# Query and key factors of the first attention: three Newton steps on DVE in place of a power on POOL

## The chip, the cores and the metric

The kernel runs on one core of a Trainium2 chip. A core has a matrix engine (PE, whose weight loads are listed as PEld), a vector engine (DVE), an activation engine (ACT), a general engine (POOL, also called GpSimd) and a queue engine (SP). Each engine works through its own list of instructions in order, and the lists are tied together by semaphores. The metric is the device time of one execution in microseconds (us), lower is better. A partition is one of 128 rows of on-chip memory; "128x24" is 24 elements in each of 128 partitions.

## The reference, cut to what matters

Two transformer-like layers run one after the other on 16 batches of 512 tokens with 128 channels. The change lies in the first attention:

```
h = rmsnorm(layernorm(x)) * norm_w
q = h @ Wq   (4 heads of 32)        k = h @ Wk   (2 heads of 32)
q = q / max(||q||, 1e-12)           k = k / max(||k||, 1e-12)      per token and head
attn = softmax(causal(q . k * exp(log_temperature)));   out = attn @ v @ Wo
x = x + xn + gate * out + experts(xn)
```

The divisions by a norm are what is touched: for each token and each of the 4 + 2 heads one factor 1/sqrt(max(sum of squares, 1e-24)) is made and multiplied in. A batch has 512 tokens in 4 tiles of 128, so the factors of a batch are a 128x24 tile. The rms norm is folded in: `r2` is its factor per token, `r2sq` its square, and the sum of squares is scaled by it first.

## The kernel before, in words

The program has six stages in a row: set-up, first attention with routing (`layer0_attention`), a table of groups, 80 groups of experts, the second attention, and again a table and groups of experts. Only the first attention is changed. It is pipelined by hand over the 16 batches `b`. Each engine has its own loop, written out in the order in which it shall work, and it is this order that decides what waits for what.

- PE in turn `b`: `scores(b, 0)` to `scores(b, 3)` (L632, L635), with the transposes and projections of batch b+2 between them; then `output(b-1)` (L658), which waits for `norm_done` from `normalise(b-1)`; `values(b, 0)` (L647); `q_columns(b+1)` (L588), which waits for `wo_used` from `add_output(b-1)`; `k_columns(b+1)`, `ranks(b+1)` (L610), and the rest of the scores and values.
- ACT in turn `b`: the exponentials of the scores, the copies of batch b+2, and last `squares(b+2)` (L523), the squares of its queries and keys.
- DVE in turn `b`: `normalise(b-1)` (a reciprocal L403 and a product `a_attnT` L405), `statistics(b+3)`, `heads_rows(b+1)` (L344: queries times factors `a_fac`), `add_output(b-1)` (L411), `choose(b+1)` (L357 to L372), `keep_sum`, `slots(b+1)` (L378 to L397), `normal_rows(b+3)` (L323, which needs `rstd` from POOL) and `square_sums(b+2)` (L336: the 128x24 sums `a_ss`).
- POOL in turn `b`: `scatter(b, 0)` (four indirect DMAs, L487), `norms(b+3)` (L458 to L464: `rstd`, `r2`, `r2sq`), `scatter(b, 1)`, and `factors(b+2)` (L474 to L479: product, maximum, power -0.5, product).

A `Chain` counts instructions of one engine: `fc.link(ins)` lets `ins` raise a semaphore and the engine wait for it before its next instruction. An instruction issued without `link` is not waited for. Where the buffers of a batch are named: `ftmp` is the scratch of the factors, `fac` the result.

Of the kernel before, what the change touches and what calls it, by code (L numbers as in the profile page):

```python
# [14 lines left out]
P = 128  # L15
# [181 lines left out]
def layer0_attention(nc, k, x_d, base_d, meta_d, xs_d):  # L197
# [4 lines left out]
    with ExitStack() as ctx:  # L202
# [11 lines left out]
        prj = sb("a_prj", [P, 2, NT, PRJ0])  # L214
        sq = sb("a_sq", [P, NT * (H0 + KV0), DH0])
        ss = sb("a_ss", [P, NT, H0 + KV0])
        ftmp = sb("a_ftmp", [P, 3, NT, H0 + KV0])
        fac = sb("a_fac", [P, NT, H0 + KV0])
        qn = sb("a_qn", [P, NT, D])
        kn = sb("a_kn", [P, NT, D])  # L220
# [37 lines left out]
        s_ps, exp_done, pv_tile = sem("a_s_ps"), sem("a_exp"), sem("a_pvt")  # L258
        norm_done, wo_ps, wo_used = sem("a_norm"), sem("a_wo_ps"), sem("a_wo_used")
        base_out = [sem(f"a_base_out{p}") for p in range(2)]  # L260
        dve_ln, dve_qkv, dve_main, pool_ln, pool_fac = (sem(f"a_{n}") for n in ("dve_ln", "dve_qkv", "dve_main", "pool_ln", "pool_fac"))

        def done(eng, sem, count):

            if count > 0:
                eng.wait_ge(sem, count)
# [5 lines left out]
        with nc.Block() as block:  # L272
# [29 lines left out]
            def _(dve):  # L302
                ln = Chain(dve, dve_ln, 1)
                heads = Chain(dve, dve_qkv, PRO_DVE_A)
                main = Chain(dve, dve_main, 1)

                def statistics(b):
                    ln.at(b)
                    dve.wait_ge(x_in[b % RX], 16 * (b // RX + 1))
                    done(dve, rstd_ready, b)  # L310
                    for t in range(NT):
                        last = nc.vector.bn_stats(stats[:, t, :], x[:, b % RX, t, :])
                    ln.link(last)
                    for t in range(NT):
                        last = nc.vector.bn_aggr(mv[:, t, :], stats[:, t, :])
                    last.then_inc(stats_ready, 1)
                    ln.end()
# [15 lines left out]
                def square_sums(b):  # L333
                    dve.wait_ge(sq_ready, b + 1)
                    done(dve, fac_ready, b)
                    nc.vector.tensor_reduce(ss[:].rearrange("p t h -> p (t h)"), sq[:], AX, ALU.add).then_inc(ss_ready, 1)  # L336

                def heads_rows(b):
                    heads.at(b)
# [34 lines left out]
                def slots(b):  # L374

                    dve.wait_ge(rank_ps, b + 1)
                    for t in range(NT):
                        nc.vector.tensor_tensor(pos[:, t], ps_p[:, RT + t * E0:RT + (t + 1) * E0], k.run0[:], ALU.add)  # L378
                        last = nc.vector.tensor_tensor(k.run0[:], ps_p[:, RT + (NT + t) * E0:RT + (NT + t + 1) * E0],
                                                       k.run0[:], ALU.add)  # L380
                        if t < NT - 1:
                            heads.link(last)
                    last.then_inc(rank_used, 1)
                    dve.wait_ge(rank_used, b + 1)
                    for c in range(2):
                        last = nc.vector.tensor_tensor(ohp[:, c], oh[:, c], pos[:], ALU.mult)
                    heads.link(last)
                    heads.link(nc.vector.tensor_reduce(slotf[:].rearrange("p c t -> p (c t)"),
                                                       ohp[:].rearrange("p c t e -> p (c t) e"), AX, ALU.add))
                    dve.wait_ge(el_ready, b + 1)  # L390
                    done(dve, meta_out[b % 2], 16 * (b // 2))
                    scatter_done(dve, b - 2)
                    heads.link(nc.vector.tensor_scalar(ep[:], el[:], 1.0, None, ALU.add))
                    wts = meta[:, b % 2].bitcast(F32)
                    heads.link(nc.vector.reciprocal(wts[:, 2 * NT:3 * NT], ep[:]))
                    nc.vector.tensor_tensor(wts[:, 3 * NT:4 * NT], el[:], wts[:, 2 * NT:3 * NT], ALU.mult)
                    nc.vector.tensor_copy(meta[:, b % 2, 0:2 * NT], slotf[:].rearrange("p c t -> p (c t)")).then_inc(meta_ready, 1)  # L397
                    heads.end()
# [17 lines left out]
                statistics(1)  # L416
                normal_rows(1)
                square_sums(0)
                statistics(2)
                heads_rows(0)  # L420
                normal_rows(2)
                choose(0)
                square_sums(1)
                slots(0)
                keep_sum(0)
                for b in range(NB):
                    if b >= 1:
                        normalise(b - 1)
                    if b + 3 < NB:
                        statistics(b + 3)  # L430
                    if b + 1 < NB:
                        heads_rows(b + 1)
                    if b >= 1:
                        add_output(b - 1)
                    if b + 1 < NB:
                        choose(b + 1)
                        keep_sum(b + 1)
                        slots(b + 1)
                    if b + 3 < NB:
                        normal_rows(b + 3)  # L440
                    if b + 2 < NB:
                        square_sums(b + 2)
                normalise(NB - 1)
                add_output(NB - 1)

            @block.gpsimd
            def _(pool):
                ln = Chain(pool, pool_ln, 6)
                fc = Chain(pool, pool_fac, 3)

                def norms(b):

                    ln.at(b)
                    pool.wait_ge(stats_ready, b + 1)
                    done(pool, xn_ready, b)
                    done(pool, fac_ready, b - 1)
                    done(pool, qkv_ready, b - 2)
                    ln.link(nc.gpsimd.tensor_scalar(tmp4[:, 0], mv[:, :, 1], EPS_LN, None, ALU.add))  # L458
                    ln.link(nc.gpsimd.tensor_tensor(rstd[:], tmp4[:, 0], k.mhalf[:, 0:NT], ALU.pow))
                    ln.link(nc.gpsimd.tensor_tensor(tmp4[:, 1], rstd[:], rstd[:], ALU.mult))  # L460
                    ln.link(nc.gpsimd.tensor_tensor(tmp4[:, 2], tmp4[:, 1], mv[:, :, 1], ALU.mult))
                    ln.link(nc.gpsimd.tensor_scalar(tmp4[:, 0], tmp4[:, 2], 1e-6, None, ALU.add))
                    ln.link(nc.gpsimd.tensor_tensor(r2[:, b % RN], tmp4[:, 0], k.mhalf[:, 0:NT], ALU.pow))
                    nc.gpsimd.tensor_tensor(r2sq[:, b % 2], r2[:, b % RN], r2[:, b % RN], ALU.mult).then_inc(rstd_ready, 1)  # L464
                    ln.end()

                def factors(b):

                    fc.at(b)
                    pool.wait_ge(ss_ready, b + 1)  # L470
                    pool.wait_ge(rstd_ready, b + 1)
                    done(pool, qkv_ready, b)
                    bc = r2sq[:, b % 2].unsqueeze(2).to_broadcast([P, NT, H0 + KV0])
                    fc.link(nc.gpsimd.tensor_tensor(ftmp[:, 0], ss[:], bc, ALU.mult))  # L474
                    fc.link(nc.gpsimd.tensor_scalar(ftmp[:, 1], ftmp[:, 0], 1e-24, None, ALU.max))
                    fc.link(nc.gpsimd.tensor_tensor(ftmp[:, 2].rearrange("p t h -> p (t h)"),
                                                    ftmp[:, 1].rearrange("p t h -> p (t h)"),
                                                    k.mhalf[:, 0:NT * (H0 + KV0)], ALU.pow))
                    nc.gpsimd.tensor_tensor(fac[:], ftmp[:, 2], r2[:, b % RN].unsqueeze(2).to_broadcast([P, NT, H0 + KV0]),  # L479
                                            ALU.mult).then_inc(fac_ready, 1)  # L480
                    fc.end()

                def scatter(b, c):
                    if c == 0:
                        pool.wait_ge(meta_ready, b + 1)
                    for t in range(NT):
                        nc.gpsimd.indirect_dma_start(  # L487
                            xs_d, bass.IndirectOffsetOnAxis(ap=meta[:, b % 2, c * NT + t:c * NT + t + 1], axis=0),
                            xn[:, b % RX, t, :], None).then_inc(scattered[b % 2], 16)

                norms(0)
                norms(1)
                factors(0)
                norms(2)
                factors(1)
                for b in range(NB):
                    scatter(b, 0)
                    if b + 3 < NB:
                        norms(b + 3)
                    scatter(b, 1)  # L500
                    if b + 2 < NB:
                        factors(b + 2)
                for p in range(2):
                    pool.wait_ge(scattered[p], SCAT * (NB // 2))

# [1489 lines left out]
```

## Time and profile before

| what | value |
|---|---|
| median of 3 runs | 1691.02 us (1690.0 to 1691.55) |
| profiled execution, its own time | 1692.21 us |
| its span (first to last instruction) | 1690.5 us |
| mean granted PE clock | 0.943 of full speed |
| busy over the span | PE 89%, DVE 69%, ACT 56%, POOL 50% |
| first attention | starts at about 12 us; its last DVE instruction ends at 351.15 us |

The busy shares are means over six stages with different limits; the change concerns only the first fifth of the span. Within it the rows of a timeline give the start of each instruction or run of instructions, how long it was, and in brackets how long its engine had been idle before it and what ended the wait.

### The profile page before, as it was taken

How to read it: one execution, taken by the hardware profiler on the slowest of the kernel's cores; microseconds unless marked ns; L12 is line 12 of the kernel's file. 1: busy time of each engine (PE TensorE's matmuls, PEld its weight loads, DVE VectorE, ACT ScalarE, POOL GpSimd, SP SyncE). 2: the span in 40 equal slices, each digit the busy share in tenths (PEclk: the TensorE clock that was granted, in tenths of full speed). 3: DMA queues.
4: the chain of work that ended last, by engine and by line, in shares of the span. 5: the costliest groups of instructions: out<-in, count | busy, mean ns of one | idle time of the engine just before them, and what ended most of it. 6: DMA issues, size and time to landing. Idle time of an engine off the chain costs nothing. (4 is left out here: it accounts for less than half of the span.)

```text
span 1690.5 us, 29816 instructions
## 1 busy us (share of the span) xinstructions
PE 1500.7 (89%) x9488; PEld 778.3 (46%) x9488; DVE 1174.4 (69%) x3105; ACT 941.4 (56%) x1805; POOL 844.9 (50%) x989
## 2 busy tenths in 40 slices
PE   3999998939996299999999999999999999639996
PEld 1444444429996133333333333333333333129996
DVE  3677777633333478989888898889988999224443
ACT  2555555514442137777777777777777777512221
POOL 4788888806001654556554655556555520104443
PEclk9999999959998559999999999999999999959998
DMA  1111111159998211122212221122211210067771
GB/s 34 50 53 51 58 57 46 52 160 277 300 299 241 68 52 47 55 75 72 62 46 62 76 61 55 56 71 75 64 52 55 67 57 5 26 214 233 237 239 64
DMA packets 141519, 165.75 MB, mean 98 GB/s; under 512 B 28010, under 2 KB 114154, under 8 KB 140138
## 3 DMA queue, kind: packets, MB, share of 16 engines
q1 hardware_dynamic: 86628, 70.75, 14.5%
q10 hardware_dynamic: 40912, 62.62, 12.0%
q0 software_dynamic: 13824, 30.47, 5.9%
q8 instruction: 78, 1.28, 0.3%
q14 instruction: 77, 0.63, 0.1%
HBM read 111.93 MB, written 51.30 MB: 97 GB/s over the span
## 5 line engine op out<-in xcount | busy, mean ns | idle before, releaser
L1529 DVE TENSOR_REDUCE c_mx<-c_ps_mx 128x1 f32<-128x512 f32 x1024 | 648.3, 682 | 86.9 <-PE c_ps_mx L1757 83.5
L1435 ACT ACTIVATE c_pt<-c_ps_e 128x512 f32<-128x512 f32 x1024 | 555.5, 602 | 198.0 <-PE c_ps_e L1729 193.5
L1757 PE MATMUL c_ps_mx<-c_kex,c_qst 72*128 72x512 bf16 x1024 | 399.4, 392 | 17.7 <-DVE c_mx L1529 9.4
L1729 PE MATMUL c_ps_e<-c_qst,c_kex 74*128 74x512 bf16 x1024 | 389.8, 383 | 1.7 <-ACT c_pt L1435 1.6
L1742 PE MATMUL c_ps_v<-c_pt,c_vp 128*32 128x512 f32 x2048 | 274.5, 608 | 1.1 <-ACT c_pt L1435 0.7
L1272 POOL DMA_INDIRECT c_gy<-ys,mt x128 | 124.3, 971 | 276.2 <-DMA mt<-meta 128.0
L1757 PEld LDWEIGHTS c_ps_mx<-c_kex,c_qst 72*128 72x128 bf16 x1024 | 100.9, 99 | 332.0 <-DVE c_mx L1529 230.0
L985 PE MATMUL f_ps_h<-f_xT,f_w 128*128 128x256 f32 x800 | 196.5, 385 | 0.0
L545 ACT ACTIVATE a_pt<-a_ps_s,temp 128x1024 f32<-128x1024 f32 (+3 forms) x128 | 113.1, 885 | 92.8 <-PE a_ps_s L635 90.4
L985 PEld LDWEIGHTS f_ps_h<-f_xT,f_w 128*128 128x128 f32 x800 | 145.4, 194 | 15.4
L487 POOL DMA_INDIRECT xs<-a_xn,a_meta x128 | 133.4, 1042 | 35.1 <-issue 32.6
L995 PEld LDWEIGHTS f_ps_y<-f_w,f_h 128*128 128x128 f32 x1120 | 144.5, 193 | 6.2
L995 PE MATMUL f_ps_y<-f_w,f_h 128*128 128x128 f32 x1120 | 144.7, 275 | 0.0
L938 POOL DMA_INDIRECT out<-f_y,f_x x80 | 76.8, 960 | 130.1 <-DVE f_y L1068 117.6
L1365 POOL DMA_INDIRECT rows<-c_row,c_bsl x64 | 64.0, 999 | 155.1 <-PE c_ps_v L1742 123.8
L1729 PEld LDWEIGHTS c_ps_e<-c_qst,c_kex 74*128 74x128 bf16 x1024 | 100.4, 98 | 72.7 <-ACT c_pt L1435 16.7
L1016 ACT ACTIVATE f_h<-f_ps_h,f_w 128x256 f32<-128x256 f32 x160 | 68.3, 474 | 88.8 <-PE f_ps_h L985 87.9
L1012 ACT ACTIVATE f_g<-f_ps_h 128x256 f32<-128x256 f32 x120 | 46.1, 384 | 120.9 <-PE f_ps_h L985 101.6
L632 PE MATMUL a_ps_s<-a_qT,a_kT 32*128 32x128 f32 (+3 forms) x512 | 108.4, 500 | 0.3
L973 PE MATMUL f_ps_x<-ident,f_x 128*128 128x128 f32 x240 | 47.3, 280 | 63.3 <-DMA f_x<-rows 39.7
L1072 DVE TENSOR_TENSOR f_y<-f_ps_y,f_w 128x256 f32<-128x256 f32 x80 | 33.9, 424 | 98.7 <-PE f_ps_y L995 98.7
L1060 DVE TENSOR_TENSOR f_h<-f_ps_h,f_g 128x256 f32<-128x256 f32 x120 | 50.9, 425 | 66.8 <-ACT f_g L1012 66.8
(225 smaller groups left out, 1898.8 us busy)
## 6 DMA issues: line engine op xcount, KB each, us to landing
f_w<-in_we ACTq DMA_DIRECT2D x80, 321.0 KB, 4.5
f_w<-in_we ACTq DMA_DIRECT2D x40, 576.0 KB, 4.4
c_qst<-qparts SPq DMA_DIRECT2D x45, 384.0 KB
f_x<-rows SPq DMA_DIRECT2D x40, 257.0 KB, 3.9
f_x<-xs SPq DMA_DIRECT2D x80, 128.0 KB, 4.6
ys<-f_y ACTq DMA_DIRECT2D x80, 128.0 KB, 4.3
qparts<-c_qp SPq DMA_DIRECT2D x16, 384.0 KB, 2.5
c_kex<-kparts SPq DMA_DIRECT2D x48, 96.0 KB
```

The costliest lines, as they stand in the source:

```text
L487: nc.gpsimd.indirect_dma_start(xs_d, bass.IndirectOffsetOnAxis(ap=meta[:, b % 2, c * NT + t:c * NT + t + 1], axis=0), xn[:, b % RX, t, :], ...
L545: nc.scalar.activation(pt[:, kt % 2, 2 * pr:2 * pr + 2, 0:n], ps_s[:, u % 2, :, 0:n], ACT.Exp, bias=k.temp[:, 3:4], scale=k.temp[:, 1:2]). ...
L632: nc.tensor.matmul(ps_s[:, u % 2, j, 0:L - kt * P], kT[r, b % 2, kt * P:(kt + 1) * P], qT[r, b % 2, kt * P:L], start=True, stop=False)
L938: nc.gpsimd.indirect_dma_start(ys_d, bass.IndirectOffsetOnAxis(ap=x[:, q, t, 2 * D:ROW].bitcast(U32), axis=0), y[:, q, t, :], None).then_i ...
L985: last = nc.tensor.matmul(ps_h[u][:, n, :], w[:, q, col:col + P], xT[:, q % 2, :], start=True, stop=True)
L995: last = nc.tensor.matmul(ps_y[q % 2][:, t * D:(t + 1) * D], h[:, q % 2, c, t * P:(t + 1) * P], w[:, q, col:col + D], start=c == 0, stop=c ...
L1272: nc.gpsimd.indirect_dma_start(gy[:, p, n, :], None, ys_d, bass.IndirectOffsetOnAxis(ap=mt[:, p, n:n + 1], axis=0)).then_inc(gathered[p], 16)
L1435: nc.scalar.activation(pt[:, s % 4, hl, :], ps_e[:, ring_bank(p, n)], ACT.Exp, scale=QSCALE).then_inc(exp_done, 1)
L1529: nc.vector.tensor_reduce(mx[:, g % 2, n % 16:n % 16 + 1], ps_mx[:, ring_bank(p, n)], AX, ALU.max).then_inc(mx_done, 1)
L1729: nc.tensor.matmul(ps_e[:, ring_bank(p, n)], kex[:, p, hl, kt * P:(kt + 1) * P], qst[:, p, HL * g + hl, :], start=True, stop=True).then_in ...
L1742: last = nc.tensor.matmul(ps_v[32 * hl:32 * (hl + 1), :], vp[:, p, kt, hl, :], pt[:, s % 4, hl, :], start=kt == 0, stop=kt == NT - 1)
L1757: nc.tensor.matmul(ps_mx[:, ring_bank(p, n)], qst[0:SROW, p, HL * g + hl, qt * P:(qt + 1) * P], kex[0:SROW, p, hl, :], start=True, stop=Tr ...
```

## The change

The four POOL instructions of `factors` go away, in the loop and twice ahead of it. Fourteen DVE instructions on 128x24 tiles take their place, right behind the sums of squares: the product with `r2sq`, the maximum, an integer guess of 1/sqrt (the bits read as an integer, times -0.5, plus a constant), the halved negative, three Newton steps of three instructions, and the product with `r2`. Each waits for the one ahead of it through a semaphore, with one exception: the halved negative is issued right behind the guess.

```diff
@@ -214,7 +214,7 @@
-        ftmp = sb("a_ftmp", [P, 3, NT, H0 + KV0])
+        ftmp = sb("a_ftmp", [P, 4, NT, H0 + KV0])
@@ -258,7 +258,7 @@
-        dve_ln, dve_qkv, dve_main, pool_ln, pool_fac = (sem(f"a_{n}") for n in ("dve_ln", "dve_qkv", "dve_main", "pool_ln", "pool_fac"))
+        dve_ln, dve_qkv, dve_main, pool_ln, dve_fac = (sem(f"a_{n}") for n in ("dve_ln", "dve_qkv", "dve_main", "pool_ln", "dve_fac"))
@@ -303,6 +303,7 @@
+                fc = Chain(dve, dve_fac, 12)
@@ -334,6 +335,26 @@
+                def factors(b):
+
+                    fc.at(b)
+                    dve.wait_ge(ss_ready, b + 1)
+                    dve.wait_ge(rstd_ready, b + 1)
+                    a, y = ftmp[:, 1], ftmp[:, 2]
+                    flat = [c.rearrange("p t h -> p (t h)") for c in (a, y)]
+                    fc.link(nc.vector.tensor_tensor(ftmp[:, 0], ss[:], r2sq[:, b % 2].unsqueeze(2).to_broadcast([P, NT, H0 + KV0]), ALU.mult))
+                    fc.link(nc.vector.tensor_scalar(a, ftmp[:, 0], 1e-24, None, ALU.max))
+                    nc.vector.tensor_scalar(flat[1].bitcast(mybir.dt.int32), flat[0].bitcast(mybir.dt.int32), -0.5, float(0x5f3759df),
+                                            ALU.mult, ALU.add)
+                    fc.link(nc.vector.tensor_scalar(ftmp[:, 0], a, -0.5, None, ALU.mult))
+                    for n in range(3):
+                        fc.link(nc.vector.tensor_tensor(ftmp[:, 3], ftmp[:, 0], y, ALU.mult))
+                        fc.link(nc.vector.tensor_tensor(a, ftmp[:, 3], y, ALU.mult))
+                        fc.link(nc.vector.scalar_tensor_tensor(y, a, 1.5, y, ALU.add, ALU.mult))
+                    nc.vector.tensor_tensor(fac[:], y, r2[:, b % RN].unsqueeze(2).to_broadcast([P, NT, H0 + KV0]),
+                                            ALU.mult).then_inc(fac_ready, 1)
+                    fc.end()
@@ -416,11 +437,13 @@
                 square_sums(0)
+                factors(0)
                 statistics(2)
                 heads_rows(0)
                 square_sums(1)
+                factors(1)
                 slots(0)
@@ -440,13 +463,13 @@
                         normal_rows(b + 3)
                     if b + 2 < NB:
                         square_sums(b + 2)
+                        factors(b + 2)
                 normalise(NB - 1)
@@ -464,22 +487,6 @@
-                def factors(b):
-
-                    fc.at(b)
-                    pool.wait_ge(ss_ready, b + 1)
-                    pool.wait_ge(rstd_ready, b + 1)
-                    done(pool, qkv_ready, b)
-                    bc = r2sq[:, b % 2].unsqueeze(2).to_broadcast([P, NT, H0 + KV0])
-                    fc.link(nc.gpsimd.tensor_tensor(ftmp[:, 0], ss[:], bc, ALU.mult))
-                    fc.link(nc.gpsimd.tensor_scalar(ftmp[:, 1], ftmp[:, 0], 1e-24, None, ALU.max))
-                    fc.link(nc.gpsimd.tensor_tensor(ftmp[:, 2].rearrange("p t h -> p (t h)"),
-                                                    ftmp[:, 1].rearrange("p t h -> p (t h)"),
-                                                    k.mhalf[:, 0:NT * (H0 + KV0)], ALU.pow))
-                    nc.gpsimd.tensor_tensor(fac[:], ftmp[:, 2], r2[:, b % RN].unsqueeze(2).to_broadcast([P, NT, H0 + KV0]),
-                                            ALU.mult).then_inc(fac_ready, 1)
-                    fc.end()
@@ -490,16 +497,12 @@
                 norms(0)
                 norms(1)
-                factors(0)
                 norms(2)
-                factors(1)
                 for b in range(NB):
                     scatter(b, 0)
                     if b + 3 < NB:
                         norms(b + 3)
                     scatter(b, 1)
-                    if b + 2 < NB:
-                        factors(b + 2)
```

DVE's list at the end of a turn, before. The names are the tiles above; `a_sq_r` is the semaphore of ACT's squares, `a_pvt` that of PE's last values.

```order
L323 TENSOR_SCALAR a_xn<-x,a_mv,a_rstd 128x128 [waits scat0_1,a_rstd_r]
L323 TENSOR_SCALAR a_xn<-x,a_mv,a_rstd 128x128 x3
L336 TENSOR_REDUCE a_ss<-a_sq 128x24 [waits a_fac_r,a_sq_r]
L403 RECIPROCAL a_rs<-a_ps_d 128x512 [waits a_pvt]
L405 TENSOR_TENSOR a_attnT<-a_ps_v,a_rs 128x512 [waits a_wo_ps,a_dve_main]
```

The same place after the change (every line number is now about 20 higher); the reduction and the first half of the new chain:

```order
L324 TENSOR_SCALAR a_xn<-x,a_mv,a_rstd 128x128 x3
L337 TENSOR_REDUCE a_ss<-a_sq 128x24 [waits a_fac_r,a_sq_r]
L346 TENSOR_TENSOR a_ftmp<-a_ss,a_r2sq 128x24 [waits a_rstd_r,a_ss_r]
L347 TENSOR_SCALAR a_ftmp<-a_ftmp 128x24 [waits a_dve_fac]
L348 TENSOR_SCALAR a_ftmp<-a_ftmp 128x24 [waits a_dve_fac]
L350 TENSOR_SCALAR a_ftmp<-a_ftmp 128x24
L352 TENSOR_TENSOR a_ftmp<-a_ftmp 128x24 [waits a_dve_fac]
L353 TENSOR_TENSOR a_ftmp<-a_ftmp 128x24 [waits a_dve_fac]
L354 SCALAR_TENSOR_TENSOR a_ftmp<-a_ftmp 128x24 [waits a_dve_fac]
```

The last three repeat twice, and then stand, still on DVE:

```order
L354 SCALAR_TENSOR_TENSOR a_ftmp<-a_ftmp 128x24 [waits a_dve_fac]
L355 TENSOR_TENSOR a_fac<-a_ftmp,a_r 128x24 [waits a_dve_fac]
L424 RECIPROCAL a_rs<-a_ps_d 128x512 [waits a_pvt]
L426 TENSOR_TENSOR a_attnT<-a_ps_v,a_rs 128x512 [waits a_wo_ps,a_dve_main]
L313 BN_STATS a_stats<-x 128x6 [waits a_rstd_r,x0_in1]
```

So fourteen instructions have moved in between the reduction and the reciprocal. POOL's list between two `norms`, before:

```order
L464 TENSOR_TENSOR a_r2sq<-a_r 128x4
L487 DMA xs<-a_xn,a_meta 135424x128 x4
L474 TENSOR_TENSOR a_ftmp<-a_ss,a_r2sq 128x24
L475 TENSOR_SCALAR a_ftmp<-a_ftmp 128x24
L476 TENSOR_TENSOR a_ftmp<-a_ftmp,mhalf 128x24
L479 TENSOR_TENSOR a_fac<-a_ftmp,a_r 128x24
L487 DMA xs<-a_xn,a_meta 135424x128 x4
```

and after, where the two runs of four scatters have become one of eight:

```order
L485 TENSOR_SCALAR a_tmp<-a_tmp 128x4
L486 TENSOR_TENSOR a_r<-a_tmp,mhalf 128x4
L487 TENSOR_TENSOR a_r2sq<-a_r 128x4
L494 DMA xs<-a_xn,a_meta 135424x128 x8
L481 TENSOR_SCALAR a_tmp<-a_mv 128x4
```

## Rows read from the trace of the kernel before

**Rows 1.** Windows: length, busy us and count of PE, PEld, DVE, ACT, POOL; clock; DMA.

```profile
80.00:300.00 220.00, 202.93 (x1610) 97.30 (x1606) 163.89 (x600) 121.35 (x191) 185.97 (x215) 0.95 0.18 54
```

**Rows 2.** Timeline of POOL, first attention: start, length, instruction.

```profile
109.86 1.53 POOL L487 DMA_INDIRECT xs<-a_xn,a_meta  x1 [0.17 <-POOL a_fac L479]
...
123.98 0.23 POOL L474 TENSOR_TENSOR a_ftmp<-a_ss,a_r2sq 128x24 f32<-128x24 f32 x1
...
129.34 1.53 POOL L487 DMA_INDIRECT xs<-a_xn,a_meta  x1 [0.17 <-POOL a_fac L479]
...
304.79 1.53 POOL L487 DMA_INDIRECT xs<-a_xn,a_meta  x1 [0.17 <-issue]
```

**Rows 3.** Groups of 80 to 300 us: busy, mean ns, idle before, releaser.

```profile
L487 POOL DMA_INDIRECT xs<-a_xn,a_meta x92 | 96.3, 1047 | 24.8 <-issue 23.0 <-POOL a_fac L479 1.8
...
L344 DVE TENSOR_TENSOR a_qn<-a_prj,a_fac 128x512 f32<-128x512 f32 x11 | 7.6, 692 | 27.3 <-POOL a_fac L479 27.3
```

**Rows 4.** Timeline of PE over parts of four turns.

```profile
131.72 0.63 PE L588 MATMUL a_ps_t<-ident,a_qn 128*128 128x128 f32 x4 [1.75 <-DVE a_bs L411]
...
139.14 1.13 PE L632 MATMUL a_ps_s<-a_qT,a_kT 32*128 32x512 f32 x4
...
151.19 0.63 PE L588 MATMUL a_ps_t<-ident,a_qn 128*128 128x128 f32 x4 [1.75 <-DVE a_bs L411]
...
161.52 1.13 PE L632 MATMUL a_ps_s<-a_qT,a_kT 32*128 32x512 f32 x4
...
167.55 1.11 PE L658 MATMUL a_ps_t<-wo,a_attnT 128*128 128x128 f32 x8
...
177.15 0.29 PE L635 MATMUL a_ps_s<-causal,ident_b 128*128 128x128 bf16 x2
...
178.80 1.13 PE L632 MATMUL a_ps_s<-a_qT,a_kT 32*128 32x512 f32 x4
```

**Rows 5.** Timeline of ACT and DVE at the end of that turn.

```profile
177.94 0.83 ACT L523 ACTIVATE a_sq<-a_prj 128x768 f32<-128x768 f32 x1
...
178.80 0.95 DVE L336 TENSOR_REDUCE a_ss<-a_sq 128x24 f32<-128x768 f32 x1
179.67 3.35 DVE L403 RECIPROCAL a_rs<-a_ps_d 128x512 f32<-128x512 f32 x1
183.05 0.69 DVE L405 TENSOR_TENSOR a_attnT<-a_ps_v,a_rs 128x512 f32<-128x512 f32 x1
```

**Rows 6.** Timeline of DVE, small instructions, linked and not linked.

```profile
132.95 0.42 DVE L367 CAST a_ixf<-a_ix 128x8 f32<-128x8 uint32 x1
...
136.41 0.17 DVE L393 TENSOR_SCALAR a_ep<-a_el 128x4 f32<-128x4 f32 x1
136.61 0.18 DVE L395 RECIPROCAL a_meta<-a_ep 128x4 f32<-128x4 f32 x1
136.82 0.16 DVE L396 TENSOR_TENSOR a_meta<-a_el,a_meta 128x4 f32<-128x4 f32 x1
136.90 0.17 DVE L397 CAST a_meta<-a_slotf 128x8 uint32<-128x8 f32 x1
```

**Rows 7.** One window, columns as in the first group.

```profile
152.00:158.00 6.00, 6.00 (x31) 2.44 (x30) 4.35 (x27) 2.32 (x5) 5.00 (x9) 0.50 0.27 80
```

**Rows 8.** Timeline of PE: three more waits for the same.

```profile
209.69 1.04 PE L588 MATMUL a_ps_t<-ident,a_qn 128*128 128x128 f32 x4 [1.75 <-DVE a_bs L411]
...
268.12 0.63 PE L588 MATMUL a_ps_t<-ident,a_qn 128*128 128x128 f32 x4 [1.74 <-DVE a_bs L411]
...
287.60 0.63 PE L588 MATMUL a_ps_t<-ident,a_qn 128*128 128x128 f32 x4 [1.95 <-DVE a_bs L411]
```

**Rows 9.** Timeline of PE and DVE at the two ends of the chain.

```profile
41.80 0.24 PE L610 MATMUL a_ps_p<-a_ohb,tri 128*128 128x64 bf16 x1 [3.57 <-DVE a_ohb L372]
...
64.48 0.95 DVE L336 TENSOR_REDUCE a_ss<-a_sq 128x24 f32<-128x768 f32 x1 [1.14 <-ACT a_sq L523]
...
320.21 1.16 PE L658 MATMUL a_ps_t<-wo,a_attnT 128*128 128x128 f32 x8
```

More of the change, by code:

```diff
@@ L448, in _ @@
                 ln = Chain(pool, pool_ln, 6)
-                fc = Chain(pool, pool_fac, 3)
                 def norms(b):
```

## The prediction

> **What bounds the kernel now.** The change touches only the first attention, so I read that stage by windows, then each engine's timeline through one turn of its loop. From 80 to 300 us PE is busy 202.9 of 220 us and POOL 186.0 [rows 1], and PE looks like the limit. The timeline says otherwise: the same scatter stands at 109.86, 129.34 and 304.79 [rows 2], which is one turn of 19.48 us and nine more in 175.45 us, 19.49 each. POOL repeats to 0.1 us whatever PE does. Of the 24.8 us of idle time ahead of its scatters 23.0 are "issue", time in which it waited for nobody [rows 3]; it is a queue that never empties. DVE waits for it, 27.3 us in 11 turns for the factors alone [rows 3], and PE is late in turn, 1.75 us at the query transposes, since what releases them stands behind `heads_rows` on DVE [rows 4]. Where PE had fallen behind and never waited, it made a whole turn in 178.80 - 161.52 = 17.28 us [rows 4]. So POOL sets 19.48 and PE could do 17.28.
>
> **What is removed.** The factor block holds POOL from 123.98 to 129.34, 5.36 us of 19.48 [rows 2]. Without it POOL needs 14.1 us a turn and drops out; DVE's wait for it goes.
>
> **What is added.** Fourteen small instructions on DVE. A linked 4-element one follows the one ahead by 0.20 to 0.21 us (136.41, 136.61, 136.82), an unlinked one by 0.08 [rows 6]. Width costs little: 0.16 us at 4 elements [rows 6], 0.69 at 512 [rows 3], so 0.18 at 24 and a linked step of 0.22. The reduction takes 0.95, but the reciprocal now starts 0.87 after it [rows 5], overlapping its end; a linked instruction can't, so the first product starts at 0.98. Then a step of 0.22, one of 0.21, 0.08 behind the unlinked guess, 0.21, nine of 0.22, and 0.10 from the last product to the reciprocal, which no longer waits: 0.98 + 0.22 + 0.21 + 0.08 + 0.21 + 1.98 + 0.10 = 3.78 from reduction to reciprocal in place of 0.87, **2.9 us more**.
>
> **Where it lies.** Not beside PE's work but on a ring. `output(b)` on PE needs `normalise(b)`, which on DVE stands behind `factors(b+2)`, which needs the sums of ACT's squares, which come last on ACT, behind the exponentials of PE's last scores of turn b; and these scores stand behind `output(b-1)`. From the undisturbed turn: output at 167.55, last scores to 177.15 + 0.29, reduction at 178.80, right behind the squares (177.94 + 0.83) [rows 4, 5], **11.25**. Reduction to reciprocal **3.78**. Reciprocal to end of product, 183.05 + 0.69 - 179.67 [rows 5], **4.07**. To PE about 0.05. Ring: **19.15 us**. Without the new instructions it is 16.2, under PE's 17.28, which is why it can't be seen now. So POOL's 19.48 gives way to a ring of 19.15: of the 5.4 us lifted from POOL hardly any comes through, and PE would wait 19.15 - 17.28 = 1.9 us each turn, at `output` instead of at the transposes.
>
> A surcharge: the cast at 132.95 took 0.42 us against 0.17 for its like [rows 6], beside a scatter of POOL. The three tensor_scalars of the chain will now run beside scatters. Bounds per turn: nothing, or 3 x 0.25 = 0.75. A hold ends with the scatter, so only an instruction that meets the last part of one can lose 0.25; I take a quarter of the upper bound, 0.2: **ring 19.35**, PE's wait about 2.0. The Trainium skill (SBUF — State Buffer, "Who interferes with whom") says that copies, casts and tensor_scalars on DVE can take a port pair shared with GpSimd, whoever comes second waiting for the other's whole instruction. The cast's row agrees in kind; by that rule, each of the three held for most of a scatter, a turn would cost some 2 us more (three times 0.7, an estimate from the mean scatter of 1.05 us, [rows 3]).
>
> **The clock.** PE's clock is granted at 1.00 (2.4 GHz) in most of the stage and 0.50 (1.2 GHz) in some stretches, as from 152 to 158 us [rows 7], right after the wait that ended at 151.19 [rows 4]. The mean of 0.95 over 220 us [rows 1] makes some 20 us at half rate: three stretches of 6 to 7 us, the others after the waits that end at 209.69 (its transposes already slowed, 1.04 us) and at 287.60 [rows 8]. After the wait at 268.12, whose transposes took 0.63 us, none came [rows 8], nor after that at 131.72 [rows 4]; of six waits of 1.7 us or more, three were followed by one. What a stretch costs: transposes to next scores take 139.14 - 131.72 = 7.42 at full rate and 161.52 - 151.19 = 10.33 after the wait with the drop [rows 4], **2.9 us**. Now it is hidden: POOL goes on, and PE skips its next wait or two, which also makes drops rarer. After the change the ring runs through PE, from output to last scores, exactly where the drop falls (just behind the wait), nothing is skipped, and each of 14 outputs (0 to 13) has a wait of 2.0. At 3 in 6 that is 7 drops: 7 x 2.9 = **20.3 us**, nothing if they stay away, 29 with ten.
>
> **Sum.** At the start the factors come up to 5.36 - 2.9 = 2.4 us sooner, and PE stands waiting for what follows them [rows 9]; behind that PE, not DVE, sets the pace up to the first normalise, so I let 1 us of it through. The reduction ahead of the first normalise then starts at 63.5 instead of 64.48 [rows 9], output(0) at 63.5 + 3.98 + 4.07 + 0.05 = 71.6, output(13) 13 rings later at 71.6 + 13 x 19.35 = 323.1, against 320.21 [rows 9]: +2.9. The last two turns have no factors and all later stages are untouched. The profiled execution took 1692.2: 1692.2 + 2.9 + 20.3 = 1715.4. It lies 1.2 above the median of the runs, so the forecast on the median is **1714 us**, 1.4% slower. "The same" means within 0.2% (3.4 us), about what a measurement of this kernel can tell from none.
>
> **Rivals.**
> - *The ring without the drops.* With a surcharge from 0 to 0.2 output(13) comes 0.1 to 2.9 us late: 1691 to 1694. For it: three of six waits had none, and one turn differs from the next only by where its wait falls. Against it: a longer wait, every turn. 13%, most of it within 0.2%.
> - *DVE is held up by POOL's scatters.* 0.75 a turn in place of 0.2 is 14 x 0.55 = 8 us more, and PE's wait grows to 2.6 us, so more drops: 1720 to 1735. For it: the cast. Against it: it was one instruction, and the chain spends most of its time in tensor_tensors. 12%.
> - *Faster: the chain is cheap.* If linked steps on the same tile overlapped as unlinked ones do, at 0.08 us, the chain would take 14 x 0.08 = 1.1, the ring 17.4, and PE would be the limit at 17.3 to 17.4: 13 x 2.1 = 27 us less, 1664; without drops it decides for faster from a step of 0.20 down (13 steps x 0.02 x 13 turns = 3.4 us), with seven only near 0.08. Against it: no linked row shows less than 0.20. 8%, with a half-way case near 1680 in it. The Trainium skill (VectorE: DVE Perf Modes, section on the TRN2 errata) has a table by which such an instruction takes 58 + 24 cycles at 0.96 GHz, 0.085 us; by it the chain would come near this rival. It says itself that the measured fixed part is higher, and the rows here are with that.
> - *The likeliest*, ring and 4 to 10 drops: 8.7 us under the forecast to 8.7 over it, 1705 to 1723, 67%.
>
> Range 1694 to 1726: it leaves out the faster rival, the lowest part of the first and the upper part of the second. Faster 0.09, same 0.10, slower 0.81.
>
> **What would show it.** POOL idle some 5 us a turn, its scatters no longer evenly spaced; no wait of DVE for `a_fac`. The period of the DVE reciprocals 19.2 to 19.4 us in a turn at full clock, about 22 in one with a drop. PE idle 2.0 us ahead of `output`, released by DVE's `a_attnT`, and none at the query transposes. The fourteen instructions 2.8 to 3.0 us from first to last. A mean PE clock of 0.88 to 0.94 from 80 to 300 us. I am wrong if the reciprocals stand under 19 us apart at full clock, if PE doesn't wait for `a_attnT`, or if the clock stays at 0.95 or above.

## The result

The changed kernel took 1715.31 us (median of 4 runs, 1712.01 to 1719.01) against 1690.51 for the kernel before in the same comparison (4 runs, 1688.66 to 1691.55): ratio 1.0149, 95% interval 1.0125 to 1.0172. It is slower by about 25 us. The profiled execution took 1714.62 us, its span 1712.9, at a mean granted PE clock of 0.936.

### The profile page after: what moved, and what is told of

Read it like the earlier page. It is cut to its first block and busy times, and to the rows that moved or that the text cites. A ratio compares the mean times of both kernels' runs of the same rounds, so it can differ in the third digit from the quotient of the medians.

```text
span 1712.9 us, 29976 instructions
## 1 busy us (share of the span) xinstructions
PE 1515.0 (88%) x9488; PEld 785.1 (46%) x9488; DVE 1214.6 (71%) x3329; ACT 938.9 (55%) x1805; POOL 762.1 (44%) x925
## 3 DMA queue, kind: packets, MB, share of 16 engines
q8 instruction: 78, 1.28, 0.3%
## 5 line engine op out<-in xcount | busy, mean ns | idle before, releaser
L494 POOL DMA_INDIRECT xs<-a_xn,a_meta x128 | 125.8, 983 | 74.4 <-DVE a_meta L418 41.8
```

The costliest lines, as they stand in the source:

```text
L494: nc.gpsimd.indirect_dma_start(xs_d, bass.IndirectOffsetOnAxis(ap=meta[:, b % 2, c * NT + t:c * NT + t + 1], axis=0), xn[:, b % RX, t, :], ...
```

## The profile after

The page of the changed kernel, busy time of each engine over the span:

```profile
PE 1515.0 (88%) x9488; PEld 785.1 (46%) x9488; DVE 1214.6 (71%) x3329; ACT 938.9 (55%) x1805; POOL 762.1 (44%) x925
```

POOL has lost 6 points of its share, and the time went up. The stage must be read, not the span. Windows of the changed kernel, columns as in [rows 1]:

```profile
80.00:300.00 220.00, 198.74 (x1497) 96.85 (x1490) 178.20 (x711) 112.10 (x180) 119.29 (x156) 0.91 0.17 51
93.00:96.00 3.00, 3.00 (x16) 0.98 (x19) 2.93 (x13) 0.40 (x1) 2.45 (x6) 0.50 0.00 0
97.00:112.00 15.00, 13.75 (x118) 6.72 (x116) 11.36 (x40) 10.20 (x16) 8.06 (x9) 1.00 0.18 56
176.00:181.00 5.00, 5.00 (x25) 2.10 (x24) 4.79 (x29) 0.40 (x1) 3.83 (x8) 0.50 0.19 52
```

In the same 220 us POOL is busy for 119.29 us instead of 185.97 [rows 1], and every engine but DVE does less work than before: PE issues 1497 matmuls instead of 1610. The clock fell from 0.95 to 0.91. The three short windows show how: half rate for a few microseconds, then full rate again.

Groups from 80 to 300 us, columns as in [rows 3]:

```profile
L494 POOL DMA_INDIRECT xs<-a_xn,a_meta x86 | 84.3, 981 | 31.1 <-issue 21.4 <-DVE a_meta L418 9.6
...
L365 DVE TENSOR_TENSOR a_qn<-a_prj,a_fac 128x512 f32<-128x512 f32 x10 | 6.6, 662 | 0.1
L481 POOL TENSOR_SCALAR a_tmp<-a_mv 128x4 f32<-128x4 f32 x10 | 5.9, 592 | 63.3 <-DVE a_mv L316 63.3
...
L347 DVE TENSOR_SCALAR a_ftmp<-a_ftmp 128x24 f32<-128x24 f32 x11 | 3.0, 269 | 0.4
```

DVE's wait for the factors, 27.3 us in [rows 3], is 0.1. POOL, which waited for nobody, now waits 6.3 us a turn for DVE's statistics. Both are what lifting the load from POOL should show. Next, PE's `output` in seven turns, the last three at the end of the stage. Columns as in [rows 4]; these rows answer to those there:

```profile
91.91 1.42 PE L661 MATMUL a_ps_t<-wo,a_attnT 128*128 128x128 f32 x8 [1.78 <-DVE a_attnT L426]
...
112.74 1.75 PE L661 MATMUL a_ps_t<-wo,a_attnT 128*128 128x128 f32 x8 [1.71 <-DVE a_attnT L426]
...
175.29 2.07 PE L661 MATMUL a_ps_t<-wo,a_attnT 128*128 128x128 f32 x8 [1.95 <-DVE a_attnT L426]
...
197.65 1.36 PE L661 MATMUL a_ps_t<-wo,a_attnT 128*128 128x128 f32 x8 [1.93 <-DVE a_attnT L426]
...
345.51 2.07 PE L661 MATMUL a_ps_t<-wo,a_attnT 128*128 128x128 f32 x8 [3.15 <-DVE a_attnT L426]
...
361.92 1.11 PE L661 MATMUL a_ps_t<-wo,a_attnT 128*128 128x128 f32 x8
374.93 1.16 PE L661 MATMUL a_ps_t<-wo,a_attnT 128*128 128x128 f32 x8 [4.21 <-DVE a_attnT L426]
```

PE's wait has moved from the query transposes to `output`, and it is there in every turn up to output(13) (345.51); output(14) at 361.92, the first with no chain ahead of it, has none. A row of eight matmuls takes 1.1 us at full clock; 1.4 to 2.1 says that the clock fell during it or had fallen before. And DVE in the turn between the first two of these rows, which answers to [rows 5]:

```profile
104.83 0.95 DVE L337 TENSOR_REDUCE a_ss<-a_sq 128x24 f32<-128x768 f32 x1 [0.83 <-ACT a_sq L526]
105.82 0.18 DVE L346 TENSOR_TENSOR a_ftmp<-a_ss,a_r2sq 128x24 f32<-128x24 f32 x1
106.04 0.18 DVE L347 TENSOR_SCALAR a_ftmp<-a_ftmp 128x24 f32<-128x24 f32 x1
106.25 0.23 DVE L348 TENSOR_SCALAR a_ftmp<-a_ftmp 128x24 int32<-128x24 int32 x1
106.34 0.17 DVE L350 TENSOR_SCALAR a_ftmp<-a_ftmp 128x24 f32<-128x24 f32 x1
...
108.51 0.18 DVE L355 TENSOR_TENSOR a_fac<-a_ftmp,a_r 128x24 f32<-128x24 f32 x1
108.61 3.35 DVE L424 RECIPROCAL a_rs<-a_ps_d 128x512 f32<-128x512 f32 x1
111.99 0.69 DVE L426 TENSOR_TENSOR a_attnT<-a_ps_v,a_rs 128x512 f32<-128x512 f32 x1
```

The ring can be added up from these two fences: output at 91.91 to reduction at 104.83 is 12.92 us, reduction to reciprocal (108.61) 3.78, reciprocal to end of product (111.99 + 0.69) 4.07, and 0.06 to the next output at 112.74: 20.83. The part that differs from the forecast is the first, 12.92 for 11.25, and it holds a stretch at half clock. In the turn from 175.29 to 197.65 that stretch is longer (the last window above) and the turn takes 22.36.

## The experiments

The theory: the chain stands between reduction and reciprocal on a ring that passes through PE, the ring takes some 19.4 us at full clock, and PE's wait of 1.7 to 2.0 us, once a turn, brings a stretch at half clock that lies on the ring. The main rival: the clock has nothing to do with it, and the added time is DVE's work itself. "Drop" below means such a stretch. All ratios are to the kernel before on the same chip.

### Filling PE's wait: fill_wait, and one matmul of filling: fill_one, fill_one_again

To the changed kernel, matmuls into the tile that `output` overwrites right after (`ps_t`) were added while PE waits for `normalise`, three in fill_wait and one in the other two (which are the same kernel):

```diff
                 def output(b):
-                    pe.wait_ge(norm_done, b + 1)
                     pe.wait_ge(xT_sb, min(b + 4, NB))
                     pe.wait_ge(kT_sb, min(b + 2, NB))
+                    if b < NB - 1:
+                        for n in range(3):
+                            nc.tensor.matmul(ps_t[:, 0:PRJ0], k.ident[:], k.w0[:], start=True, stop=True)
+                    pe.wait_ge(norm_done, b + 1)
```

> The changed kernel with three idle multiplications (128x272, identity by the projection weights, into the buffer that output() overwrites) issued on PE ahead of each of the waits for a_attnT but the last; they replace about 1.7 us of the wait by work and change no result. Theory (a ring of 19.15 to 19.35 us, and beyond it clock drops that the waits bring about): the turn stays at 19.2 to 19.4, the granted clock stays at 1.00 through the stage, and the time falls from 1715 to 1691 to 1696. Rival A (the drops come anyway, from the stage's lower load or from elsewhere): clock 0.91 from 80 to 300 us and 1713 or more. Rival B (the loss isn't the clock but DVE and POOL holding each other up): reciprocals still 20.8 us apart, 1713 or more.

> The changed kernel with one idle multiplication (about 0.55 us) ahead of each wait for a_attnT, in place of the three of the first run. The ring is unchanged at 19.4; PE's wait falls to about 1.3 us. Two Newton steps left a wait of 1.28 and still had nine drops of 15 turns. If idle time alone decides: again some 7 to 10 drops at 1.4 us each, 1706 to 1711. If the clock only needs a little more activity than the changed kernel gives: 0 to 3 drops, 1696 to 1700.

> One idle multiplication once more: one drop in thirteen turns the first time, at a wait of the same 1.28 us as with two Newton steps. If the shorter activity ahead of the wait makes the difference, again 0 to 3; if it was chance, more.

fill_wait: 1696.49 us, ratio 1.0052 (1.0035 to 1.0069). Its window from 80 to 300 us, two outputs from PE's timeline, and DVE between them:

```profile
80.00:300.00 220.00, 211.46 (x1692) 106.78 (x1692) 192.59 (x768) 121.06 (x193) 130.52 (x170) 1.00 0.18 55
```

```profile
91.39 1.16 PE L664 MATMUL a_ps_t<-wo,a_attnT 128*128 128x128 f32 x8 [0.51 <-DVE a_attnT L426]
...
110.82 1.16 PE L664 MATMUL a_ps_t<-wo,a_attnT 128*128 128x128 f32 x8 [0.50 <-DVE a_attnT L426]
```

```profile
102.70 0.95 DVE L337 TENSOR_REDUCE a_ss<-a_sq 128x24 f32<-128x768 f32 x1 [0.90 <-ACT a_sq L526]
...
103.90 0.37 DVE L347 TENSOR_SCALAR a_ftmp<-a_ftmp 128x24 f32<-128x24 f32 x1
...
106.69 3.35 DVE L424 RECIPROCAL a_rs<-a_ps_d 128x512 f32<-128x512 f32 x1
```

From 80 to 300 us the clock is 1.00 and no drop is left. (One came later, from 325.8 us, behind output(13) at 324.60, which had waited 1.71 us in spite of the filling.) Matmuls that compute nothing gave back 16 to 19 of the changed kernel's 25 us (1.0149 - 1.0052 of 1690 us, or 1715.31 - 1696.49); that is the share of the drops, and the rival, by which all of it is DVE's work, is out. What remains is the ring at full clock: 11.31 + 3.99 + 4.07 + 0.06 = 19.43 us, with 0.2 in the 3.99 from one tensor_scalar that took 0.37 instead of 0.18.

fill_one: 1700.4 us (1694.52 to 1703.22), 1.0060 (1.0036 to 1.0083). Up to 300 us its waits are 1.26 to 1.39 us, mostly 1.28, and its profile has one drop behind twelve waits; the single run of fill_one_again, 1698.04 us, waits 1.19 to 1.43 us, mostly 1.42, and has three. Each has one more behind output(13), where the wait was 2.6 us. So one filling matmul already avoids most of the drops, not all, and of what was expected the second case came about: the length of the idle time alone does not decide.

### The same kernel again: changed_again

> The changed kernel once more, to see whether a clock drop follows every output() again: 12 to 14 drops from 60 to 350 us if the waits bring them about, fewer than 10 if the first profile was a chance.

1714.08 us, clock 0.91, and again a drop at each of outputs 0 to 13, eleven short and three long. The count is not chance: 14 of 14, twice. Not every drop begins behind its wait. In windows of 0.1 us the clock falls between 1.2 us behind and 0.9 us ahead of the start of `output`, so some fall while PE still waits, and the last one here falls at 341.0 us, 1 us before PE's wait of 2.81 us for output(13) (344.77) began.

### What bounded the kernel before: cheap_pow

```diff
-                                                    k.mhalf[:, 0:NT * (H0 + KV0)], ALU.pow))
+                                                    k.zeros[:, 0:NT * (H0 + KV0)], ALU.mult))
```

This is the kernel before, not the changed one, and its factors are zero.

> The kernel before, with POOL's power replaced by a product with a tile of zeros: the factors are all zero, so queries and keys are, and the output is not the reference's; what is left out is POOL's 4 us of power. Theory (POOL's queue of 19.48 us was the limit of the stage, PE could do 17.28 and the ring without a chain is 16.2): turns of 17.3 us, 12 x 2.2 = 26 us less, 1663 to 1670. Rival (PE or DVE was the limit and POOL merely full): 1685 to 1691.

1658.57 us, 0.9825 (0.9809 to 0.9842). PE's timeline:

```profile
102.20 1.11 PE L658 MATMUL a_ps_t<-wo,a_attnT 128*128 128x128 f32 x8
...
119.48 1.11 PE L658 MATMUL a_ps_t<-wo,a_attnT 128*128 128x128 f32 x8
```

A turn is 17.28 us, which is what [rows 4] gave for a PE that never waits, and there is no wait in front of `output`. POOL's pow was the bound, and some 31 us (1689.77 - 1658.57) can be had by taking it off POOL, if what replaces it stays off the ring. That PE multiplies zeros here doesn't explain the pace: the kernel before made the same 17.28 with its own numbers.

### The chain at another place: factors_late

```diff
                     if b + 3 < NB:
                         statistics(b + 3)
+                    if b >= 1 and b + 1 < NB:
+                        factors(b + 1)
                     if b + 1 < NB:
                         heads_rows(b + 1)
...
                     if b + 2 < NB:
                         square_sums(b + 2)
-                        factors(b + 2)
```

The same fourteen instructions, moved behind the next `normalise` and `statistics`.

> The changed kernel with the same fourteen instructions on DVE, called one place later: behind normalise() and statistics() of the next turn, just ahead of heads_rows() that needs them. Theory (it is the place in the ring that costs, not DVE's 2.9 us of work): output() no longer waits for the chain (ring 16.2), a second ring through add_output and the query transposes comes to about 17.9 us, PE waits some 0.6 us, no clock drops; 13 turns of 17.9 in place of 20.8: 1668 to 1680. Rival (DVE has no room for 2.9 us more a turn, wherever they stand, or POOL and DVE collide): 1700 to 1715.

1683.11 us (10 runs, 1678.7 to 1689.73), 0.9968 (0.9952 to 0.9983). The work on DVE is the same as in the changed kernel, and 32 us of the time are gone (1715.31 - 1683.11): what cost so much was the place, from which PE's long waits and the drops follow. But I had expected 1668 to 1680. PE's timeline, then DVE's:

```profile
112.34 0.63 PE L592 MATMUL a_ps_t<-ident,a_qn 128*128 128x128 f32 x4 [1.12 <-DVE a_bs L432]
...
130.99 0.63 PE L592 MATMUL a_ps_t<-ident,a_qn 128*128 128x128 f32 x4 [1.13 <-DVE a_bs L432]
```

```profile
117.39 1.11 DVE L324 TENSOR_SCALAR a_xn<-x,a_mv,a_rstd 128x128 f32<-128x128 f32 x4
119.55 0.95 DVE L337 TENSOR_REDUCE a_ss<-a_sq 128x24 f32<-128x768 f32 x1 [1.06 <-ACT a_sq L527]
120.42 3.35 DVE L424 RECIPROCAL a_rs<-a_ps_d 128x512 f32<-128x512 f32 x1
123.80 0.69 DVE L426 TENSOR_TENSOR a_attnT<-a_ps_v,a_rs 128x512 f32<-128x512 f32 x1
```

PE waits at the query transposes again, and a turn is 18.65 us. Now the ring runs from there through the squares, reduction, reciprocal, product, statistics, chain and `heads_rows` back to PE. DVE is idle 1.06 us in front of the reduction, and behind it everything queues. The wait of 1.12 us brought no drop; the clock is 1.00.

### Statistics elsewhere as well: late_and_statistics and statistics_early

Both start from factors_late. The first moves `statistics` behind `choose`; the second makes it one turn earlier, at the end of the turn, where DVE was idle. This is the second, against the changed kernel, so that it holds the move of the factors too:

```diff
                 keep_sum(0)
+                statistics(3)
                 for b in range(NB):
                     if b >= 1:
                         normalise(b - 1)
-                    if b + 3 < NB:
-                        statistics(b + 3)
+                    if b >= 1 and b + 1 < NB:
+                        factors(b + 1)
...
                     if b + 3 < NB:
                         normal_rows(b + 3)
+                    if b + 4 < NB:
+                        statistics(b + 4)
                     if b + 2 < NB:
                         square_sums(b + 2)
-                        factors(b + 2)
```

> The kernel with the factors late, and statistics() moved too, from behind normalise() to behind choose(), so that it no longer stands between the reciprocal and what releases PE's query transposes. Theory: the second ring, measured at 18.64 us with the factors late, loses the 1.2 us of statistics() and comes to 17.4, and PE's own 17.3 is the limit; no drops; 13 turns x 1.3 = 17 us under the kernel with the factors late: 1664 to 1670. Rival (POOL's norms, now released later, hold up normal_rows): DVE waits for a_r2sq and the time stays at 1680 or above.

late_and_statistics: 1682.03 us, 0.9949 (0.9932 to 0.9967), a miss. A group of 80 to 300 us shows the wait that took the place of the one removed:

```profile
L324 DVE TENSOR_SCALAR a_xn<-x,a_mv,a_rstd 128x128 f32<-128x128 f32 x48 | 15.0, 370 | 12.7 <-POOL a_r2sq L489 12.7
```

`normal_rows` needs what POOL makes of the statistics; with the statistics later, DVE waits for POOL, 12.7 us over twelve turns, which is the rival on record. The turn stays at 18.7 us (PE's outputs at 106.66 and 125.35).

> The kernel with the factors late, and statistics() of the batch after next moved from behind normalise() to the end of the turn before, ahead of square_sums(), where DVE waits 1.06 us for ACT's squares. POOL gets its numbers earlier, not later. Theory: the second ring, 18.64 us, loses 1.2 us and gains at most 0.2 at the squares: 17.4 to 17.7 a turn, no drops, 13 turns x 1.0 to 1.2 under the 1683 of the kernel with the factors late: 1667 to 1671, 1.2% under the kernel before the change. Rival (another wait takes its place, as in the run with the statistics behind choose): 1678 or more.

statistics_early: 1670.37 us (5 runs, 1666.3 to 1672.59), 0.9864 (0.9845 to 0.9884), faster than both kernels. Its window, and two outputs of PE:

```profile
80.00:300.00 220.00, 214.82 (x1758) 103.95 (x1754) 204.64 (x818) 133.12 (x209) 141.74 (x181) 1.00 0.20 59
```

```profile
85.70 1.11 PE L663 MATMUL a_ps_t<-wo,a_attnT 128*128 128x128 f32 x8
103.19 1.11 PE L663 MATMUL a_ps_t<-wo,a_attnT 128*128 128x128 f32 x8
```

17.49 us a turn, 0.2 from PE's own 17.28, no wait in front of `output`, clock 1.00. DVE is busy for 204.64 of 220 us.

### Fewer and more steps: newton_one, newton_two, newton_two_again, late_four_steps

`range(3)` in `factors` becomes 1 or 2 in the changed kernel, or 4 in factors_late, which changes how often the three instructions of a step repeat and how precise the factors are.

> The changed kernel with one Newton step (it leaves out the last two refinements). The ring at full clock was 19.43 with three steps and 18.78 with two; with one 18.13, PE's wait about 0.65 us. No drops expected at such a wait: output(13) at about 69.5 + 13 x 18.13 = 305, 15 us ahead of the kernel before, so 1674 to 1678. Rival (drops still come from lower activity ahead of output): 1680 or more.

> The changed kernel with two Newton steps instead of three (it leaves out the last refinement of the factors). Theory: the ring is 3 x 0.217 = 0.65 us shorter, 18.5; PE's wait falls from 1.9 to about 1.2 us, a length after which the kernel before never had a drop (0.7, 1.0 and 1.1 us): output(13) at about 70.4 + 13 x 18.5 = 311 in place of 320 in the kernel before, so 1679 to 1685, which is faster than before the change. Rival (drops come after any wait of DVE, in proportion): 14 x 0.65 = 9 us only, 1706.

> Two Newton steps once more (it leaves out the last refinement): nine drops in fifteen turns the first time. If the count is a matter of how the waits fall in time, it will differ, between 4 and 12.

> The kernel with the factors late and four Newton steps (one more than it needs): PE's wait at the query transposes grows from 1.13 to about 1.8 us, as long as the waits at output() in the changed kernel, and the turn at full clock to 19.3, nearly as long too (19.43). It asks what brings the clock drops. If it is the length of the wait: one in nearly every turn, 14 of them, and about 1712. If it is also what PE does ahead of it (values and full-height scores here, the narrow scores ahead of output()): at most half of the turns, as in the kernel before, 1690 to 1703.

newton_one: 1675.03 us, 0.9916 (0.989 to 0.9943), as expected: turns of 17.93 (86.88 to 104.81) or, with a held tensor_scalar, 18.14, waits of 0.4 to 0.65 us, clock 1.00 from 80 to 300 us.

newton_two missed: 1692.47 us, 1.0026 (1.0011 to 1.0041), where 1679 to 1685 was expected. Two outputs:

```profile
70.00 1.16 PE L661 MATMUL a_ps_t<-wo,a_attnT 128*128 128x128 f32 x8 [1.08 <-DVE a_attnT L426]
...
88.77 2.08 PE L661 MATMUL a_ps_t<-wo,a_attnT 128*128 128x128 f32 x8 [1.28 <-DVE a_attnT L426]
```

At full clock the turn is 18.77 us, 0.66 under fill_wait's 19.43 (each with one held tensor_scalar), so three instructions are worth 0.66 us: 0.22 each, as linked steps were priced. I had expected that waits of 1.1 to 1.3 us bring no drops; up to 350 us nine came, and seven in newton_two_again (1694.45 us), and they ate the gain. The nine are of the slowest of its six runs (1699.9 us), so that its median run may well have had fewer.

late_four_steps: 1713.15 us, 1.0123 (1.0099 to 1.0147). PE's timeline:

```profile
97.35 1.06 PE L592 MATMUL a_ps_t<-ident,a_qn 128*128 128x128 f32 x4 [1.79 <-DVE a_bs L432]
...
183.77 0.63 PE L592 MATMUL a_ps_t<-ident,a_qn 128*128 128x128 f32 x4 [1.78 <-DVE a_bs L432]
```

The wait is at the transposes, as in the kernel before, but in every turn. Up to 350 us eleven drops came, as at 97.35 (1.06 us for four transposes instead of 0.63), and none behind 183.77. The three added instructions of about 0.22 us account for some 8 us over 12 turns; the other 22 that lie between its median and factors_late's came with the drops.

What PE's wait was, how many such waits there were and how many drops began, all from 60 to 300 us, where every kernel is in its regular turns ("again" is the second profile of the same kernel):

| kernel | PE's wait in a turn, us | waits | drops | clock, 80 to 300 us |
|---|---|---|---|---|
| cheap_pow, statistics_early | none | - | 0 | 1.00 |
| newton_one | 0.4 to 0.65 | 13 | 0 | 1.00 |
| fill_wait | 0.45 to 0.51 | 12 | 0 | 1.00 |
| factors_late | 1.12, once 1.38 | 12 | 0 | 1.00 |
| late_and_statistics | 1.15 | 12 | 0 | 1.00 |
| fill_one; again | 1.26 to 1.39; 1.19 to 1.43 | 12; 12 | 1; 3 | 0.99; 0.98 |
| newton_two; again | 1.06 to 1.29; 1.07 to 1.29 | 12; 12 | 7; 6 | 0.94; 0.95 |
| kernel before | 0.7 to 1.95 | 9 | 3 | 0.95 |
| late_four_steps | 1.78 | 11 | 9 | 0.91 |
| changed kernel; again | 1.7 to 1.95 | 11; 11 | 11; 11 | 0.91; 0.91 |

Past 300 us the faster kernels are in their last turns, with other work for PE, and there a drop can come with no wait of PE in its timeline. Two windows of cheap_pow, columns as in [rows 1]:

```profile
303.00:306.00 3.00, 2.84 (x16) 0.82 (x12) 2.55 (x2) 2.93 (x3) 2.39 (x3) 0.94 0.15 49
306.00:309.00 3.00, 3.00 (x16) 2.12 (x18) 0.31 (x1) 1.11 (x2) 2.08 (x4) 0.50 0.17 49
```

PE was busy for 2.84 of the 3 us in which the clock began to fall. statistics_early has the same at 312.4 us, and in newton_one the clock fell at 300.1 us, 1.4 us before PE began to wait for the output at 302.72. So waits bring drops, but not they alone.

## Why the prediction was right, and where it was off

**POOL's bound and its removal: right.** The factor block left POOL, its wait-free queue became one with 6.3 us of waiting a turn, and DVE's wait for `a_fac` went. cheap_pow shows the other half, that PE then could do 17.28.

**The chain's 3.78 us: right to the hundredth** (104.83 to 108.61), the fourteen instructions 2.87 us from first to last. The rival in which linked steps overlap at 0.08 us is out: the rows stand 0.21 to 0.22 apart. By the formula for a float32 tensor_tensor that the Trainium skill gives (VectorE: DVE Perf Modes, section on the TRN2 errata), checked there at 512 and 2048 elements, one of 24 elements is estimated at (24 + 151) cycles at 0.96 GHz, 0.182 us; the rows show 0.18. The same section's table would give 0.085, and the rows contradict it.

**The ring: right.** Forecast 19.35 with the surcharge, measured 19.43 at full clock in fill_wait, with all four pieces as forecast (11.31 for 11.25, 4.07 for 4.07). PE's wait came to `output`, released by `a_attnT`, 1.7 to 1.95 us for the forecast 2.0 (3.15 at output(13)).

**The surcharge for scatters: in kind right, smaller in the changed kernel.** Means over 80 to 300 us, against 0.18 when nothing holds them: L347 0.269 and L348 0.214 in the changed kernel, some 0.13 a turn together; L347 0.360 in fill_wait, which is the forecast 0.2. What decides is where in a scatter the instruction falls. POOL's scatters, in the changed kernel beside the chain shown above and in fill_wait beside its own:

```profile
105.55 0.95 POOL L494 DMA_INDIRECT xs<-a_xn,a_meta  x1 [0.30 <-issue]
```

```profile
103.34 0.96 POOL L494 DMA_INDIRECT xs<-a_xn,a_meta  x1 [0.30 <-issue]
```

In the first, L347 ran from 106.04 to 106.22 in the midst of the scatter and took its 0.18, and L348 behind it took 0.23 and ended at 106.48, with the scatter (106.50). In the second, L347 began at 103.90, 0.56 behind the scatter's start, took 0.37 and ended at 104.27, with the scatter (104.30). Over four profiles (the changed kernel, changed_again, fill_wait, newton_two_again) each held one ends with its scatter, and none took more than 0.42. So a hold does end with the scatter, as assumed. The Trainium skill (SBUF — State Buffer, "Who interferes with whom") lets a tensor_scalar be held for the whole of GpSimd's instruction; L347 in the first scatter contradicts that, as only the last third or so of a scatter holds here.

**The drops: the mechanism right, number and price mis-sized.** This is the term that was off: "7 x 2.9". There were 14, not 7: from three drops after six waits (five of them in [rows 4, 8]) I took a chance of one half for each wait, where a wait in every turn brought one in every turn. And most were shorter than those before: twelve cost 12.92 - 11.31 = 1.6 us each, two cost 3.1 (22.36 - 20.83 = 1.5 more). The sum, 12 x 1.6 + 2 x 3.1 = 25.4 us, is not far from 20.3, so that the total held because two errors of about a factor of two, in opposite directions, nearly cancelled. That was luck. Taken over whole turns, the 13 up to output(13) needed 13 x (21.12 - 19.43) = 22 us more than those of fill_wait at full clock. The measured time would have been met about as well by a wrong count as by the right one; only the trace tells them apart.

**The sum.** Output(0) came at 70.99 for 71.6, output(13) at 345.51 for 323.1 + 20.3 = 343.4: 13 turns of 21.12 us. Output(15) is at 374.93, in the kernel before at 348.28, 26.6 us later; the first matmul of the expert stage comes 25.3 us later (400.39 for 375.1), and the profiled executions end 22.4 us apart. The 2.9 us between these two were regained in later stages that the change does not touch. At the last scores of the second attention the lag is 24.1 us (1485.6 for 1461.5) and at the first indirect write of the last expert stage 22.4 (1541.5 for 1519.1), so some 1.2 us came back up to the former and 1.7 between the two. The cause is open, and the forecast had no such term. Had they not been regained, the profiled execution would have ended 2 us above the forecast 1715.4, not 0.8 under it.

**What stays open.** What, besides a wait, brings a drop. The ends of the table are clear: none in 49 waits of four kernels, all but one of them up to 1.15 us, and one at every wait of 1.7 to 1.95 us in the changed kernel. In between the length does not order them: newton_two_again has drops at waits of 1.10 and 1.13 us (88.63, 108.87), and fill_one_again waits longer than newton_two_again, mostly 1.42 against 1.08 us, and has half the drops. Part of the gap may be the choice of execution, one profile each, fill_one's of the fastest of its four runs and newton_two's of the slowest of its six. That the place of the wait alone decides is refuted, since late_four_steps has its 1.78 us at the transposes and nine drops behind eleven waits; why the kernel before had three behind six waits as long at the same place is open. So is why some drops last twice as long (6.8 us for 3.4): in the changed kernel and its repeat the long ones are those that began earliest, 0.7 us or more before `output` could start, as at 174.6 for 175.29.

## What to carry to other kernels

Before moving work from a saturated engine to one with idle time, find the ring (engine to engine and back within a turn) and ask on which side of it the work lands; 2.9 us between two instructions of the ring cost the kernel 25 us, and the same instructions elsewhere in the turn gained 5 to 7, and 20 to 23 once the work that they then delayed had been put into DVE's idle time. When the change leaves PE waiting once a turn for as long as here, 1.7 to 1.95 us, price a stretch at half clock for every turn, and read from the trace whether it lies on the ring. If the wait can't be removed, a few matmuls into a tile that is about to be overwritten can be cheaper than waiting: here three saved 16 to 19 us.

## What the runs showed of the hardware

- PE fell to half clock in each of the 14 turns with a chain of the changed kernel, at waits of 1.7 to 1.95 us (the last 3.15), one a turn of 21 us. With the waits cut to 0.50 us the granted clock was 1.00 from 80 to 300 us.
- Twelve of these stretches took 3 to 4 us, as the one that the window from 93 to 96 us lies in, and two took 6 to 7, as in the kernel before [rows 7].
- A stretch at half clock can begin while PE has work: from 303 to 306 us of cheap_pow it was busy for 2.84 us, and from 306 to 309 the clock was 0.50.
- On DVE an instruction of 24 elements that waits for the one ahead through a semaphore follows it by 0.21 to 0.22 us, some 0.04 us after its end; the unlinked one follows by 0.09 (106.25, 106.34).
- A tensor_scalar of 24 elements on DVE ran at its 0.18 us in the midst of one of POOL's scatters (106.04 within 105.55 to 106.50) and was held to the scatter's end, for 0.37 us, where it met the last part of one (103.90 within 103.34 to 104.30).
